# Weights of six attention heads kept in a PSUM bank during the third layer's gather

## The reference, cut to what matters

```python
h = x @ W                                     # one head, 64 features
score = s_src[src] + s_dst[dst]
edge_e = jnp.exp(-jax.nn.leaky_relu(score, 0.2))
rowsum = segment_sum(edge_e, src)
msg = segment_sum(edge_e[:, None] * h[dst], src)
h_prime = msg / (rowsum[:, None] + 1e-16)
```

## Time and profile before

| | us |
|---|---|
| median of 3 runs | 5101.0 |
| lowest and highest run | 5093.85, 5111.67 |
| profiled execution | 5096.59 |
| its span | 5094.9 |
| gather stage, first weighing to last add | 3514.0 to 4172.9 |

### The profile page before, as it was taken

The page is one execution under the profiler, slowest core; times in us unless marked ns, Lnnn a source line. Parts: engine busy times, 40 slices in busy tenths (PEclk is TensorE's granted clock), DMA queues, the critical chain, the costliest instruction groups (busy, mean ns, idle before and its releaser), DMA issues. The chain is left out here.

```text
span 5094.9 us, 46821 instructions
## 1 busy us (share of the span) xinstructions
PE 1668.8 (33%) x10711; PEld 940.9 (18%) x10711; DVE 2834.9 (56%) x4778; ACT 1642.0 (32%) x4317; POOL 2028.2 (40%) x1847
## 2 busy tenths in 40 slices
PE   4133200100000000001544334521222218899989
PEld 3022200100000000000111111110111117744444
DVE  5728567781777779870433333452777766722131
ACT  1322300110655666000544334511444446310010
POOL 0055777706777710037123444126777731000000
PEclk9566555555555555555666656665555559999999
DMA  3000000005666610002011121215787834577756
GB/s 120 19 12 1 3 1 1 1 3 166 170 180 186 184 38 0 0 22 52 18 37 48 50 58 53 60 47 187 236 257 244 255 91 127 189 287 265 271 169 212
DMA packets 211351, 550.13 MB, mean 108 GB/s; under 512 B 46145, under 2 KB 109179, under 8 KB 210372
## 3 DMA queue, kind: packets, MB, share of 16 engines
q0 software_dynamic: 99984, 272.83, 19.7%
q1 hardware_dynamic: 111156, 274.90, 15.8%
HBM read 484.06 MB, written 63.56 MB: 107 GB/s over the span
## 5 line engine op out<-in xcount | busy, mean ns | idle before, releaser
L1167 POOL DMA_INDIRECT blend_got<-rec,blend_slot x416 | 396.2, 953 | 538.0 <-DVEq L1210 405.9
L896 POOL DMA_INDIRECT table<-edges_record,edges_place x391 | 517.0, 1322 | 144.2 <-issue 128.2
L2695 PE MATMUL fourth_bank<-fourth_tile,fourth_z 128*128 128x512 f16 (+1 forms) x2800 | 559.8, 361 | 19.9 <-DVEq L2856 10.1
L2065 POOL DMA_INDIRECT heads_got<-rec,heads_slot x416 | 469.1, 1128 | 181.6 <-issue 123.7
L244 PE MATMUL blend_count<-blend_mov,blend_stat 128*128 x980 | 353.8, 445 | 559.9 <-issue 467.9
L1603 POOL DMA_INDIRECT sum_got<-rec,sum_slot x416 | 455.1, 1094 | 158.8 <-issue 124.9
L1219 DVE TENSOR_SCALAR blend_mov<-built_iota_low,built_low 128x800 f16 x490 | 213.4, 436 | 516.1 <-issue 327.0
L1677 DVE TENSOR_TENSOR rounds_y<-rounds_y,sum_got 128x516 f32 x416 | 291.0, 700 | 124.0 <-issue 34.3
L1247 ACT ACTIVATE blend_gap<-built_iota_ten,built_offset 128x128 f32 x490 | 197.1, 402 | 494.6 <-issue 409.4
L200 PE MATMUL edges_p_key<-kept_ident,edges_key_row 128*128 128x128 f32 x4 | 1.1, 428 | 1036.0 <-DVEq L167 1036.0
L2695 PEld LDWEIGHTS fourth_bank<-fourth_tile,fourth_z 128*128 128x128 f16 x2800 | 261.5, 99 | 311.9 <-issue 15.4
(11 more groups left out here) (666 smaller groups left out, 4419.0 us busy)
## 6 DMA issues: line engine op xcount, KB each, us to landing
fourth_tile<-cs SPq DMA_DIRECT2D x100, 800.0 KB, 4.5
fourth_tile<-ct SPq DMA_DIRECT2D x100, 800.0 KB, 4.3
ct<-blend_cst SPq DMA_DIRECT2D x20, 1000.0 KB
heads_counts<-ct SPq DMA_DIRECT2D x25, 800.0 KB
cs<-heads_flipped SPq DMA_DIRECT2D x25, 800.0 KB
attend_cnt<-ct SPq DMA_DIRECT2D x50, 256.0 KB, 2.7
sort_low_wide<-low SPq DMA_DIRECT2D x4, 3136.0 KB
attend_cnt<-ct SPq DMA_DIRECT2D x25, 288.0 KB, 3.2
```

The source lines that it names most:

```text
L896: pool.indirect_dma_start(table, bass.IndirectOffsetOnAxis(ap=K["place"][0:lanes, t:t + 1], axis=0), K["record"][0:lanes, t, :], None).the ...
L1167: pool.indirect_dma_start(got[:, buf, r, :], None, rec_dram, bass.IndirectOffsetOnAxis(ap=slot[:, t:t + 1], axis=0)).then_inc(gathered[buf ...
L2065: pool.indirect_dma_start(got[:, buf, r, :], None, rec_dram, bass.IndirectOffsetOnAxis(ap=slot[:, t:t + 1], axis=0)).then_inc(gathered[buf ...
L2695: last = pe.matmul(bank[m][:, 0:w], z2[s % 2][:, k, part, :], tile[:, n % RING, at:at + w], start=(k == 0 and part == 0), stop=(k == NB - ...
```

## The change

The masked weights of VectorE's six heads no longer go back to `heads_factor` in SBUF, but to `p_slot` in PSUM, in three parts for the three buffers (3 x 13 x 6 = 234 floats of the bank's 512). `scale` reads its weights there. ScalarE's two heads stay in `heads_factor`. So `mask` now has two instructions, of 78 and of 26 elements a partition.

```diff
+    there = heads - ON_ACT
+    across = p_slot[:, 0:BUFS * ROWS * there].rearrange("p (u r h) -> p u r h", u=BUFS, r=ROWS)
...
                 e = factor[:, n % BUFS, :, :]
                 dve.wait_ge(exped, n + 1)
-                step(dve.tensor_tensor(e, e, live[:, n * ROWS:(n + 1) * ROWS].unsqueeze(2).to_broadcast([P, ROWS, heads]), ALU.mult))
+                alive = live[:, n * ROWS:(n + 1) * ROWS].unsqueeze(2)
+                step(dve.tensor_tensor(across[:, n % BUFS, :, :], e[:, :, ON_ACT:heads], alive.to_broadcast([P, ROWS, there]), ALU.mult))
+                step(dve.tensor_tensor(e[:, :, 0:ON_ACT], e[:, :, 0:ON_ACT], alive.to_broadcast([P, ROWS, ON_ACT]), ALU.mult))
                 dve.sem_inc(factors, 1)
...
-                dve.tensor_tensor(part, part, factor[:, buf, r, ON_ACT:heads].unsqueeze(2).to_broadcast([P, heads - ON_ACT, F1]),
+                dve.tensor_tensor(part, part, across[:, buf, r, :].unsqueeze(2).to_broadcast([P, there, F1]),
                                   ALU.mult).then_inc(scaled, 1)
```

## The result

The changed kernel took 5129.7 us (median of 8 runs, 5122.5 to 5135.9), the kernel before beside it 5099.6 us (8 runs, 5088.5 to 5111.7). The ratio is 1.0060, with a 95% interval of 1.0047 to 1.0073: **slower by 0.6%**, 30 us. The prediction said 5106 in a range of 5088 to 5134.

A forecast was written before the change was run, and what follows sets the result against it. VectorE's own order was taken to bound the gather stage (652 of 659 us). Mask +5.9, PSUM read 0 and GpSimd's relief -1 gave +4.9 on the profiled 5096.6, 5106 us against the median; range 5088 to 5134.

The forecast's parts named there:

- The likeliest case: Whole kernel: 5106 us, +0.1%, within the 0.3% that counts as no change; chance 0.74.
- rival (a): VectorE's weighing from PSUM loses its overlap with the add: 0.083 us more a row, 34.5 us, 5141 us; chance 0.16.
- The prediction's own sign of being wrong: Gather stage: the sum of VectorE's idle time before adds changes by more than 15 us, among other signs.
- Part 1, the mask: VectorE's mask in two instructions, 233 and 180 ns: 0.59 us where 0.41 stood, +5.9 us over 32 sets.
- the bound of 2.7 us for that write: First mask instruction's write to PSUM: taken as 0, at most 0.083 us later a set, 2.7 us over 32.
- Part 2, the PSUM read: VectorE's 416 weighings read PSUM: 0 to 8.3 us in all, taken as 0, overlap with the add kept.
- Part 3, GpSimd: Gathers' mean falls from 1135 to 1050 ns, 35 us hidden in longer waits for freed sets; 1 us gained.
- the prediction's first guess: In the gather stage, the weighing's second SBUF operand holds up GpSimd's gathers; without it their mean falls to 1050 ns.
- rival (c): GpSimd's gathers get no relief, something else holding them: forecast plus 1, 5107 us; chance counted within the forecast's 0.74.
- the sum, +5.9 - 1: Whole kernel: mask cost less GpSimd's gain, +4.9 us on the profiled 5096.6, so 5101.5.
- rival (b): GpSimd's relief halves VectorE's 54.6 us idle before adds: -27 + 5.9 = -21 us, 5080 us; chance 0.10.
- its bad side: Tighter gathers may push the count tiles back: +10 to +20 us, counted within the slack of the forecast.

The follow-up runs named there:

- the split kernel: Changed kernel with the six heads' weights in an SBUF tile of their own instead of PSUM, mask still in two instructions: 5050.5 us, 0.9988 of the kernel before.
- the kernels with fewer products: Most degree-count products left out on TensorE: changed kernel 0.9992 on third and fourth chip; kernel before 0.9998 and 1.0003, each against the unaltered kernel before.
- The memset of 115 elements: Changed kernel with a 115-element memset behind each gather on GpSimd, fourth chip: 4393.0 us, 0.9999 of the kernel before.
- the small memset: Changed kernel with a one-element memset on GpSimd behind each of the 416 gathers, second chip: 5112.7 us, 1.0119 of the kernel before.
- the row-by-row waits: GpSimd waits before each gather for one row's add, not a whole set: changed kernel 5095.4 us (1.0079), kernel before 5065.4 us (1.0021).

## Why the prediction was right, and where not

**The time** of 5129.7 lies in the range, near its upper end, and the direction was right. The likeliest case was not what happened: it put the time within 0.3% of before, and it came 0.6% above. That the range held is luck: its upper end was set for rival (a), which did not happen, and the time came there by another way. The prediction's own sign of being wrong came true: the sum of the idle time before adds changed by 20.3 us, beyond the 15 it named, and the stage took 680.7 us instead of about 664.

**Part 1, the mask:** right. 233 and 180 ns were forecast, 240 and 187 measured; 0.59 us to the weighing, measured 0.60; +5.9 us, measured 6.1. The instruction that writes PSUM lasted 240 ns and the same one into SBUF 230 (in the split kernel), so the bound of 2.7 us for that write was wide enough: it is 0.3 us.

**Part 2, the PSUM read:** right, and so rival (a) is wrong. The weighing keeps its overlap with the add (0.471 us from start to start, against 0.475), and lasts 552 to 557 ns over all kernels instead of 557 to 560, a little below 0 where the prediction saw nothing point. (It counted four rows with a PSUM operand in the earlier trace rows; three have one, and L2477 is the SBUF fellow of L2475.) The slow case was given 0.16 for this mechanism, and it ended slow for another. The fixed cost which the Trainium skill gives a PSUM source ("VectorE: DVE Perf Modes", section on the TRN2 errata) would by that estimate have been 27 us here. It doesn't appear: the instruction is 5 ns shorter than its SBUF form.

**Part 3, GpSimd:** the relief came, and was larger than forecast (1013 ns instead of 1050; 114.9 us of waiting instead of 85). A gather begun under a weighing fell from 1254 to 946 ns, as the prediction's first guess, the second SBUF operand, has it, and so rival (c) is wrong. The Trainium skill's rule that a VectorE instruction with two SBUF inputs contends with a GpSimd instruction that reads SBUF ("SBUF — State Buffer", Who interferes with whom) agrees with that. Mis-sized was its use. I took 1 us; the waits for gathered rows fell by 2.1 us on the first chip (6.3 to 4.2), and by 3.5 and 6.2 us on the third and fourth, in the kernels with fewer products.

**The step that failed** is the sum, +5.9 - 1, which leaves the 54.6 us of idle time before adds as they were, at a change of 0, without a reason. I gave half of them to rival (b) as a gain, and let its bad side, "+10 to +20 us", vanish in the slack of the forecast, without a chance of its own. It was +20.3 us, two thirds of the result. And I looked for a cause of the 54.6 us only in ScalarE, held by TensorE. The rows before the adds said `issue` for 31.6 of them, which is time in which the profile sees nobody to wait for, and I did not look at what the other engines did in those moments. The slow stretches stood in the trace of before, on three engines at once.

**What is shown:** the change's own instructions cost nothing on a chip without slow stretches (0.9994). The split does not bring the loss (0.9988). On the two chips with slow stretches the loss is there only in kernels that read PSUM (1.0060; 5095.4 against 5065.4 us), and most of it stands as idle time before adds.

**What is open:** whether the PSUM read lengthens the slow stretches itself, or through the quicker gathers that it allows. The memset of 115 elements was to tell, and ran where there was nothing to lengthen. What a slow stretch is, is open too. Several engines at once issuing an instruction only now and then, while gathers run, looks like a shortage of instructions. No row shows an engine waiting for its code. The traces do list the packets of two DMA queues of the kind `instruction`: 44 in the stage before the change, 44 after it and 44 in the changed kernel on the fourth chip, where nothing is slow, and the longest took 1.6, 1.7 and 2.2 us. So they were neither more nor longer on the chip with slow stretches; whether one came late, the list doesn't tell. Whether the recording of the trace has a part in the stretches was not tried either. The Trainium skill ("Runtime: NRT & Kernel Launch", Instruction fetch mechanics) says that each sequencer fetches its instructions in blocks through a DMA queue of its own, which would fit with a shortage, and no run here tests it.

## What to carry to other kernels

Idle time with no named releaser is a term of the sum like any other. If several engines show it at once, look at all of them in those moments, price a change in it, up and down, and give the bad side a chance. Moving one operand of a two-operand VectorE instruction into PSUM freed GpSimd here without slowing VectorE, and gave back only what VectorE had waited for gathers, 2 to 6 us. After such an edit, look in the trace whether it did what it was meant to do: the small memset and the row-by-row waits did not. Before an experiment of half a per cent is believed, have the unaltered change beside it on the same chip.

## What the runs showed of the hardware

A VectorE product with its second operand in PSUM, one weight read over for 65 elements, is as fast as from SBUF (552 to 557 against 557 to 560 ns for 390 elements).

GpSimd's indirect gathers lasted 0.95 us (median) where VectorE was idle or had just begun a weighing with one SBUF operand, 1.25 where they began under a weighing with two, and 1.36 to 1.39 where they began under an add, which has two. A memset of 0.12 us between two of them is free, since 0.30 us lie between their work anyway. With 115 elements it takes 0.21 us and moves them apart.

Behind the load of 13 registers VectorE stood idle for 0.62 to 0.64 us in set 0, for 1.27 to 1.36 us in the sets 4, 8, 12 and so on (the row at 3862.36), and for 3.12 or more in all others (the row at 3867.64 in the earlier trace rows), in all fourteen traces, with four exceptions of 2.4 to 2.8 us among the sets 4, 8, 12 and so on, all of them on the chips with slow stretches. Only in set 0 and in the sets 4, 8, 12 and so on does the place of the 13 words, 52 bytes a set, come to a multiple of 16 bytes from the tile's start. That this is the reason was not tried.

The same program took 5100, 5056, 4396 and 4395 us on four chips. The changed kernel's gather stage took 681 us on the first and 607 us on the fourth, where it began 658 us earlier. The largest part of that lies in an earlier stage, which the change doesn't touch: its 416 gathers took 924 us from the first to the last on the first chip and 544 on the fourth. The gathers themselves lasted about the same, 951 and 970 ns, but GpSimd stood idle between them for 538.3 us in one and 149.9 in the other, the first chip first:

```profile
L1167 POOL DMA_INDIRECT blend_got<-rec,blend_slot x416 | 395.8, 951 | 538.3 <-DVEq L1210 405.9
```

```profile
L1167 POOL DMA_INDIRECT blend_got<-rec,blend_slot x416 | 403.3, 970 | 149.9 <-issue 125.6
```

So the difference between two chips is many times what the change does, and it is there in a stage without the change too. What differs between the chips is open.
